# Folding the router of a mixture-of-experts layer into the attention's output projection

## What is computed

```python
x = x + tanh(g_xattn) * attention(layernorm(x), ctx, ...)        # wq, bq, ..., wo, bo; 16 heads, 77 keys
x = x + tanh(g_ffn)  * ffn(layernorm(x), Wr, br, ln_g, ln_b, W1, b1, W2, b2)

# ffn(xt):
router_logits = xt @ Wr + br                                     # 256 x 8
gates = max(softmax(router_logits)); idx = argmax(router_logits)
xn = (xt - mean(xt)) * rsqrt(var(xt) + 1e-5) * ln_g + ln_b       # a second layernorm
y = (relu(xn @ W1[idx] + b1[idx]) @ W2[idx] + b2[idx]) * gates   # one expert for each token
```

## Time and profile before

| | us |
|---|---|
| median of 3 runs | 321.33 |
| the 3 runs | 319.93, 321.33, 322.99 |
| the profiled execution | 319.76 |
| span of its profile, first to last instruction | 317.9 |

### The profile page before, as it was taken

One profiled execution on the slowest core, in us unless ns is written; L12 is line 12 of the kernel. 1 busy time (PEld: TensorE's weight loads), 2 busy tenths in 40 slices (PEclk: granted clock), 3 DMA queues, 4 the chain that ended last, 5 costly groups with the idle time before them and its releaser, 6 DMA issues.

```text
span 317.9 us, 7719 instructions
## 1 busy us (share of the span) xinstructions
PE 281.4 (89%) x2490; PEld 251.9 (79%) x2490; DVE 199.4 (63%) x647; ACT 169.6 (53%) x456; POOL 124.1 (39%) x240
## 2 busy tenths in 40 slices
PE   6877999989999999998627999999999999999980
PEld 2657888778788888888513999889899989999970
DVE  4376789999898999878784563343434543344540
ACT  2240767777777777765323586525345824555440
POOL 2425145555555555433514536212132444332220
PEclk9595999999999999999956799999999999999996
DMA  6999991000003654451124121111111111212210
GB/s 154 277 325 372 381 371 39 36 36 35 36 1 104 219 206 164 176 162 40 37 102 118 38 84 57 53 35 54 53 57 52 52 50 53 69 51 74 64 56 15
DMA packets 19849, 34.61 MB, mean 109 GB/s; under 512 B 2517, under 2 KB 14609, under 8 KB 19798
## 3 DMA queue, kind: packets, MB, share of 16 engines
q1 hardware_dynamic: 15509, 21.28, 20.5%
q0 software_dynamic: 4144, 12.62, 12.9%
q10 hardware_dynamic: 144, 0.07, 0.1%
HBM read 27.60 MB, written 6.75 MB: 108 GB/s over the span
## 4 chain that ended last, share of the span: by engine, by line
PE 65%; DVE 17%; issue 6%; ACT 4%; POOL 2%; DMA 2%; SPq 1%; DVEq 1%; POOLq 0%; ACTq 0%
PE pS L1654 21%; PE pB L1725 15%; PE pB L1447 6%; DVE mx L858 4%; PE pA L1354 4%; PE pT L1354 3%; PE pS L1403 3%; DVE Pb L866 3%; PE pB L1472 2%; DMA cst<-in_consts_dram 2%; ACT QT L548 2%; PE pS L1349 1%; PE pA L1382 1%; PE pT L1382 1%; DVE st L892 1%
## 5 line engine op out<-in xcount | busy, mean ns | idle before, releaser
L1654 PE MATMUL pS<-znf,W1c 128*128 128x128 f32 x576 | 72.3, 280 | 0.5 <-DVE W1c L1237 0.4
L1654 PEld LDWEIGHTS pS<-znf,W1c 128*128 128x128 f32 x576 | 68.6, 195 | 3.7 <-issue 3.7
L1725 PE MATMUL pB<-W2p,hT 128*128 128x256 f32 x408 | 53.7, 286 | 0.0
L1258 DVE TENSOR_SCALAR hA<-pS,b1s 128x128 f32<-128x128 f32 x72 | 20.3, 344 | 52.1 <-PE pS L1654 42.5
L1725 PEld LDWEIGHTS pB<-W2p,hT 128*128 128x128 f32 x408 | 50.0, 190 | 1.4 <-issue 1.2
L399 POOL DMA_INDIRECT out_dram<-yo,idxs x17 | 17.6, 1037 | 72.9 <-DVE yo L1286 63.9
L733 ACT ACTIVATE hA<-pS,b1s 128x128 f32<-128x128 f32 x72 | 20.5, 368 | 46.4 <-PE pS L1654 46.4
L1447 PEld LDWEIGHTS pB<-VB,PT 128*128 128x128 f32 (+1 forms) x320 | 36.9, 192 | 3.0 <-issue 2.1
L1447 PE MATMUL pB<-VB,PT 128*128 128x51 f32 (+1 forms) x320 | 38.3, 275 | 0.6 <-DVE xs L887 0.5
L858 DVE TENSOR_REDUCE mx<-pS 128x8 f32<-128x616 f32 x32 | 25.4, 793 | 6.2 <-PE pS L1403 4.2
L554 ACT ACTIVATE Pb<-Pb 128x616 f32<-128x616 f32 x32 | 23.0, 720 | 9.9 <-DVE Pb L866 9.9
(11 more groups left out here) (229 smaller groups left out, 497.2 us busy)
## 6 DMA issues: line engine op xcount, KB each, us to landing
W1s<-in_L_ffn_W_dram SPq DMA_DIRECT2D x8, 1024.0 KB, 8.8
W2s<-in_L_ffn_W_dram SPq DMA_DIRECT2D x8, 1024.0 KB, 10.5
rows_dram<-pay POOLq DMA_DIRECT2D x16, 260.0 KB, 2.8
xs<-in_x_dram SPq DMA_DIRECT2D x3, 512.0 KB, 8.1
W2s<-in_sel_dram SPq DMA_DIRECT2D x1, 385.0 KB
zin<-rows_dram,idxg POOLq DMA_INDIRECT x21, 3.4
out_dram<-yo,idxs POOLq DMA_INDIRECT x17
W1s<-in_L_xattn_wk_dram SPq DMA_DIRECT2D x1, 256.0 KB, 3.2
```

Of the source, the lines that this page charges most:

```text
L1654: t = e.matmul(pS[:, 2 * (s % 2) + n, 128 * c:128 * c + 128], W1c[k][n][:, 128 * c:128 * c + 128], znf[s % 2][:, 128 * k:128 * k + 128], s ...
L1725: t = e.matmul(o, hT[s % 2][a][:, 128 * c:128 * c + 128], W2p[b_][c // 2][:, D * (c % 2):D * (c % 2) + D], start=False, stop=(c == 7 and a ...
```

## The change

The router's logits are rewritten. With r the inverse standard deviation of x2 and C the matrix Wr less its column means, layernorm(x2) @ Wr = r * (x2 @ C), and x2 @ C = x @ C + tanh(g) * (attention @ (wo^T C) + bo @ C). So:

- `wrc` = Wr less its column means. PE makes the means with a matmul ahead of the tile loop (`pe_wrm`), DVE subtracts them.
- `woR` = wo^T C, eight columns beside the transposed wo (`wT["wo"]` is now 264 wide, DX = 264). PE computes it in pass 1 behind the transposes of wo, with bo @ C: six matmuls in fp32 (12 instructions of 8 columns). ACT copies wo, woR and bo @ C out with three instructions, the first of which now waits for the last of these matmuls.
- x @ C: `route(i)` now multiplies the transposed normalised x by `wrc`, one tile ahead (`route(n+1)` at the end of pass n; `route(0)` and `route(1)` at the end of pass 0). DVE's `x_logits` multiplies by the standard deviation of x (which POOL now computes with one more operation in `rstd1`), adds bo @ C, and puts it into columns 256 to 263 of `xs`. `route(1)` waits on `dve_xg`, that is for `x_logits(0)`.
- `project` is 264 wide and `resid` adds 264 columns; `logits` is one DVE operation on these 8 columns. It needs no matmul, and comes at tile n-2; `router`, `gate`, `gate_exp` and `store_row` are at n-3 instead of n-4.
- Gone: `normed2`, the tile `xl`, `transpose_xl`, half of the copy to XX. `z_row` now makes z from `xs` with a scale and a bias, which POOL's `rstd2` computes (five operations instead of six).
- Behind the last tile the order on PE, ACT and DVE is new; both last projections go to pB, and `attend(z)` waits for `resid(y)`.
- SP: the loads of Wr and br are issued before that of wv; one small load of bo is added; `bmask` shares a semaphore with `sel`, and PE waits for both.

```diff
@@ SP
             load_x(1, 2)
+            e.dma_start(wrs[:, :, :], Wr.rearrange("(k p) e -> p k e", p=128)).then_inc(d["rt"], 16)
+            e.dma_start(brb[:, :], br.partition_broadcast(128)).then_inc(d["rt"], 16)
             load_w("wv")
...
+            e.dma_start(brow2[4:6, :], bo.rearrange("(k p) -> k p", p=128)).then_inc(d["ln"], 16)
@@ POOL
                 e.tensor_tensor(mv1[:, j, 3:4], mv1[:, j, 2:3], mhalf, ALU.pow).then_inc(g["pool_r1"], 1)
+                e.wait_ge(g["pool_r1"], i + 1)
+                e.tensor_tensor(mv1[:, j, 2:3], mv1[:, j, 2:3], mv1[:, j, 3:4], ALU.mult).then_inc(g["pool_sd"], 1)
@@ ACT
                 if n == 1:
-                    e.wait_ge(g["pe_wT"], 4)
+                    e.wait_ge(g["pe_wT"], 5)
                     e.wait_ge(g["act_tg"], 1)
-                    e.activation(wT["wo"][:, :, :].rearrange("p k d -> p (k d)"), bank["T1"], ACT.Copy,
+                    e.activation(wT["wo"][:, :, 0:D], bank["T1"].rearrange("p (k d) -> p k d", k=2), ACT.Copy,
                                  scale=tg[:, 0:1]).then_inc(g["act_wT"], 1)
+                    e.activation(wT["wo"][:, :, D:DX], pA[:, 256:272].rearrange("p (k d) -> p k d", k=2), ACT.Copy,
+                                 scale=tg[:, 0:1]).then_inc(g["act_wT"], 1)
+                    e.activation(boR[:, :], pA[:, 272:280], ACT.Copy, scale=tg[:, 0:1]).then_inc(g["act_wT"], 1)
@@ DVE
-            def normed2(i):
...
+            def x_logits(i):
+                e.wait_ge(g["pe_lg"], i + 1)
+                e.wait_ge(g["pool_sd"], i + 1)
...
+                    e.scalar_tensor_tensor(out=o, in0=a, scalar=sd, in1=boR[:, :], op0=ALU.mult,
+                                           op1=ALU.add).then_inc(g["dve_xg"], 1)
...
             def logits(i):
-                e.wait_ge(g["pe_lg"], i + 1)
+                e.wait_ge(g["pool_r"], i + 1)
...
-                e.tensor_tensor(Lg[:, i % 2, 0, :], bank["T1"][:, 0:E], brb[:, :], ALU.add).then_inc(g["dve_lg"], 1)
+                e.scalar_tensor_tensor(out=Lg[:, i % 2, 0, :], in0=xs[:, i, D:DX], scalar=mv2[:, i % 4, 3:4],
+                                       in1=brb[:, :], op0=ALU.mult, op1=ALU.add).then_inc(g["dve_lg"], 1)
...
+                if n == 2:
+                    e.wait_ge(g["act_wT"], 6)
+                    e.wait_ge(g["dve_xg"], 2)
+                    e.tensor_tensor(xs[:, 0:2, D:DX], xs[:, 0:2, D:DX], boR[:, :].unsqueeze(1).broadcast_to([128, 2, E]),
+                                    ALU.add).then_inc(g["dve_own"], 1)
...
-                if n >= 4:
-                    together(router(n - 4))
+                if n >= 3:
+                    together(router(n - 3))
...
                 if n == 0:
                     e.wait_ge(g["pe_ln"], 1)
-                    e.tensor_copy(bcol[:, 4:8], pB[:, 0:4]).then_inc(g["dve_lnb"], 1)
+                    e.tensor_copy(bcol[:, 4:10], pB[:, 0:6]).then_inc(g["dve_lnb"], 1)
+                    x_logits(0)
...
-                if n >= 3:
-                    logits(n - 3)
+                if n >= 2:
+                    logits(n - 2)
+                if n + 1 < NT:
+                    x_logits(n + 1)
 
             y, z = NT - 2, NT - 1
             e.wait_ge(g["pool_iota"], 1)
             early = rank(0)
-            third = (p for p, _ in zip(early, range(13)))
-            together(router(y - 2), third)
+            together(router(y - 1))
+            resid(y)
+            stats2(y)
+            for _, _ in zip(range(9), early):
+                pass
             norm(z)
-            gate(y - 2)
-            logits(y - 1)
+            gate(y - 1)
+            logits(y)
+            together(router(y))
+            resid(z)
+            stats2(z)
             for _ in early:
                 pass
...
             gate(y)
             logits(z)
             together(router(z), rank(1))
@@ PE
+            for k in range(2):
+                t = e.matmul(pB[:, 128:136], vm[:, 18:19].broadcast_to([128, 128]), wrs[:, k, :], start=(k == 0),
+                             stop=(k == 1))
+            t.then_inc(g["pe_wrm"], 1)
...
                 if n == 1:
                     e.wait_ge(g["act_PT"], 2)
                     weight("wo", "T1")
+                    e.wait_ge(g["act_Q"], 5)
+                    for k in range(2):
+                        for m in range(2):
+                            e.matmul(pA[:, 256 + 8 * k:264 + 8 * k], wr4["wo"][:, m, 128 * k:128 * k + 128],
+                                     wrc[:, m, :], start=(m == 0), stop=(m == 1))
+                    for m in range(2):
+                        t = e.matmul(pA[:, 272:280], boc[:, m:m + 1].broadcast_to([128, 128]), wrc[:, m, :],
+                                     start=(m == 0), stop=(m == 1))
+                    t.then_inc(g["pe_wT"], 1)
...
+                if n == 0:
+                    route(0)
+                if n + 1 < NT:
+                    route(n + 1)
...
+            def route(i):
+                e.wait_ge(g["act_XX"], i + 1)
+                if i >= 1:
+                    e.wait_ge(g["dve_xg"], i)
+                if i == 2:
                     e.wait_ge(g["act_wT"], 4)
...
             ranks(0)
-            for grp in range(3):
-                transpose_P(z, grp)
...
+            transpose_O(y)
+            transpose_P(z, 0)
+            project(y)
+            transpose_P(z, 1)
+            transpose_P(z, 2)
             attend(z)
-            transpose_O(y)
-            project(y)
-            route(y - 1, NT + 2)
             counts(0)
-            e.wait_ge(g["dve_On"], NT)
             transpose_O(z)
             project(z)
```

More of the change, by code:

```diff
@@ L27 @@
 NC = 10
+DX = D + E
 HK = H * LK
@@ L642, in _ @@
                     x2_row(n - 2)
-                if n >= 4:
-                    gate_exp(n - 4)
+                if n >= 3:
+                    gate_exp(n - 3)
                 for step in (0, 2, 4):
@@ L1125, in _ @@
             early = rank(0)
-            third = (p for p, _ in zip(early, range(13)))
-            together(router(y - 2), third)
-            norm(z)
-            gate(y - 2)
-            logits(y - 1)
+            together(router(y - 1))
[3 more added lines that the diff above has]
+                pass
+            norm(z)
+            gate(y - 1)
[3 more added lines that the diff above has]
+            stats2(z)
             for _ in early:
                 pass
-            resid(y)
-            stats2(y)
-            together(router(y - 1))
-            normed2(y)
-            resid(z)
-            stats2(z)
-            gate(y - 1)
-            logits(y)
-            normed2(z)
-            together(router(y))
             gate(y)
@@ L1381, in query @@
                     for k in range(2):
-                        t = e.matmul(o, wT["wq"][:, k, 128 * m:128 * m + 128], XX[:, k, :], start=(k == 0),
-                                     stop=(k == 1))
+                        t = e.matmul(o, wT["wq"][:, k, 128 * m:128 * m + 128], XX[:, 2 * (i % 2) + k, :],
+                                     start=(k == 0), stop=(k == 1))
                     t.then_inc(g["pe_Q"], 1)
```

241 lines of the change are left out of this document (103 added, 138 removed).

## The result

The changed kernel takes 325.31 us (median of 6 runs, 323.05 to 330.81), the kernel before beside it 319.97 (median of 6). The ratio is 1.020, with a 95% interval of 1.015 to 1.024: it is slower by 2% (the two medians stand at 1.017), where +0.6% was forecast. On the scale of the prediction that is 321.33 x 1.0198 = 327.7 us, outside its range of 319.8 to 326.2. The profiled execution took 324.86 us, with a span of 323.0 against 317.9.

What follows compares the result with a forecast made beforehand. A ring of dependent PE and DVE steps, 7.58 us a pass, was taken as the bound. Terms for the loop's passes and the stage behind the last tile were summed as +1.85 on 321.33: 323.2 us, range 319.8 to 326.2.

Steps and rivals of the forecast that it cites:

- The ring and the transposes: Tile loop: `attend` waits for `resid`, 0.15 behind its end, so removing the transposes of `xl` is worth 0.
- Pass 0, +1.2: `route(1)` and `scores(1)` wait for `x_logits(0)`, so VB starts about 1.4 later; +1.2 us left, bounds 0.6 and 2.1.
- If the clock rises at the same time as before: Pass 0: low clock still ends at 31.9, so transposes of P run at full clock, 0.9 instead of 1.7 us.
- rival (a): Passes 0 and 1: the clock's rise moves with the later dense work, costing 1.7 us more: 324.9 us; chance 0.25.
- Pass 1, +2.4: Transposes of wo to `scores(2)`: 12 small matmuls, ACT's copy and `route(2)` make 3.0 instead of 0.62 us; +2.4.
- Pass 2, +0.2: Adding `bo @ C` two tiles ahead of `resid(0)` puts one small operation on the ring; +0.2 us.
- Pass 3, +1.25: Router of tile 0 now runs here, delaying ACT's bias and query copies and the maximum of tile 4; +1.25 us.
- a part of the -0.3: Loop, passes 4, 6 and 8: DVE's work gets shorter by about 0.1 a pass; -0.3 us, between 0 and -0.6.
- the price of the new `logits`: DVE in the loop: the new 8-column operation was taken at 0.2 us, bounds 0.10 and 0.41.
- The stage behind the last tile, -2.9: After the loop: `logits(15)` comes at about 157.5 instead of 160.38; -2.9 us, bounds 2.1 and 3.8.
- wider rows: Loop: the projection and `resid` grow from 256 to 264 columns; 0.01 a pass, some 0.1 us in all.

Runs made afterwards that it cites:

- the run with four edits: Changed kernel with eight useless matmuls in pass 0, wo's copy before a wait, POOL's sum behind row stores, Q's copy first: 315.11 us, ratio 0.990.
- the kernels with three edits: Changed kernel with wo's work in pass 0, POOL's sum later, Q's copy first: 310.8 to 320.8 us; with three useless matmuls too: 312.5 to 321.9.

## Why the prediction was wrong

**The ring and the transposes: right.** `attend` stands 0.15 behind `resid`, the pass takes 7.59, and putting two transposes back costs nothing. The total of the prediction is out by 0.1, however: its terms add up to +1.95, not +1.85, and those of the loop to 4.85.

**Pass 0, +1.2: the work right, the clock wrong.** Measured is +2.31 (17.46 against 15.15). At full clock it is 13.63 - 12.36 = 1.27, where the prediction had about 1.4. The other 1.04 is clock: 3.83 lost in the changed kernel, 2.79 in the kernel before. The step that failed is "If the clock rises at the same time as before". It rose at 33.5, which is 34.9 in the times of before (whose scores(0) start 1.4 later), against 31.9, and past the 33 that rival (a) named as its condition. Rival (a) has the price about right (1.7, where 1.04 was measured; the stretch is 10.2 us long instead of 6.8), and the reason wrong. It had the rise move because dense work starts later. PE was dense again from 23.93, 25.3 in the times of before and no later than the 25.7 of the prediction, and the clock stayed low for 9.6 us from there, where it had been 6.3 before. That filling the idle time removes the stretch is shown; why it is longer than before is not. That `scores(1)` no longer stood in the idle time does not explain it: with the scores back ahead of the wait the stretch was as long.

**Pass 1, +2.4: right.** Measured is +2.80 (6.54 against 3.74 from `attend(0)` to `scores(2)`), at full clock 6.35 - 3.77 = 2.58. The twelve matmuls took 1.40 (1.3 in the sum, and 0.3 by the 25 ns of the Trainium skill, TensorE: Matmul & The Clock Gate, section "Wait — 56ns, not 53.3ns?", with which the trace does not agree), and PE's wait for the copy 0.87 (0.8). The run with the copy first shows that 1.0 of it was the order of one wait on ACT.

**Pass 2, +0.2: work +0.3, and a clock that no step had.** 7.91 - 7.59 = 0.32 is what is left with the stretch of low clock gone; that stretch costs 0.68. The prediction had said PE would idle for 0.8 there, and had asked of the clock only in pass 0.

**Pass 3, +1.25: right**, 1.13, of which 0.88 goes with Q's copy ahead of the bias copies.

**Pass 4: a clock that no step had.** Of its +1.00, 0.97 is the stretch of low clock behind the idle 1.30 that pass 3's wait leaves in front of `scores(4)`; the run with POOL's sum moved, in which the clock held there, took 8.12 (8.09 before).

**Passes 5 to 10, a part of the -0.3: wrong in sign.** They took 50.22 against 49.16, +1.06. The step that failed is the price of the new `logits`: its row was looked for by size ("the smallest operations"), not by where its inputs lie. It moved its first input from PSUM to SBUF, and in six passes had to wait for a sum on POOL that had been harmless. With that sum moved, they take 48.97: the contention is worth 1.25, and of the expected gain 49.16 - 48.97 = 0.19 is there.

**The stage behind the last tile, -2.9: the order right, the number in part luck.** `logits(15)` came 19.29 behind the scores of tile 15, where 157.5 - 138.8 = 18.7 was worked out. In six of the twelve profiles with the new order it comes at 18.08, so the order is worth 21.60 - 18.08 = 3.5. In the changed kernel's profile 1.2 of it is lost to the clock, of which the prediction asked nothing here: the last projection took 2.12 and its transposes 0.69, and 1.16 and 0.44 in the run with four edits. Then 0.53 came back behind `logits(15)`, where no change was forecast and where the twelve profiles differ by 3.3.

**The ledger** of the loop's +9.33, as the differences above give it (the forecast of 5.05 has pass 0 with its help from the clock; at full clock it would be 5.3):

| | forecast | measured |
|---|---|---|
| added work and waits in passes 0 to 3, measured at full clock | 5.05 | 3.85 + 0.32 + 1.13 = 5.30 |
| more low clock in passes 0 to 2, and in pass 4 | 0 | 1.26 + 0.68 + 0.97 = 2.91 |
| DVE in passes 4 to 10 | -0.3 | 0.03 + 1.06 = 1.09 |
| wider rows | 0.1 | 0.03 |
| sum | 4.85 | 9.33 |

The forecast of the added work and waits was out by at most 0.25. Nearly all of the loop's miss of 4.48 is in two couplings that a sum of parts does not hold: what an idle time does to the clock of the work behind it, and what an operation on one engine does to one on another. Four things stay open: why the stretch of pass 0 is 10.2 us long and not 6.8 as before, what makes the clock fall while PE is busy in the kernels with three edits, why it falls in passes 9 and 10 of three runs, and why it held behind the idle 1.30 in two profiles of eight. That the stretches of passes 0 and 2 go with idle time is shown, as filling or removing the idle time removed them.

## What to carry to other kernels

When a change puts a wait into a dense stretch, price the clock with it as a possible loss (here 0.7 to 3.8 us each time), and do so at every place where the sum itself says that the engine idles, not at the largest alone. Try to move work into such idle time rather than behind it: here the same instructions cost 3.85 us in one place (1.0 of it by the order of a wait) and 0.6 in the other. Then take many executions, since the kernels that did so had long ones too, 1 of 4, 8 of 12 and 4 of 8, and the kernel with the work in its old place and four edits had none in 6. When an operand moves from PSUM to SBUF, look at what POOL does at that moment, and keep DVE operations with two SBUF inputs away from it, even the smallest.

## What the runs showed of the hardware that was not expected

- Useless work can pay: eight matmuls of 1.89 us in an idle stretch made the kernel 4.4 us shorter from tile 0 to 15.
- An operation of 8 columns takes as long as the 256-column sum on POOL that it meets, 0.38 to 0.77 instead of 0.22, when both its inputs are in SBUF. Its forerunner, with one input in PSUM, took 0.16 in the midst of the same sum. Started 0.03 ahead of the sum it took 0.22, and the sum 0.78 instead of 0.72.
- The clock fell behind idle times of PE of 0.87, of 1.05 and in six profiles of 1.30 us, held behind the same 1.30 in two, and fell for 17 us in a kernel whose PE was busy for most of the time.
- Twelve small fp32 matmuls, each with a stationary operand of its own, took 1.40 us, 0.12 each.
